# A two-layer graph kernel on 4096 nodes: the adjacency matrix is turned by VectorE's 32x32 transpose, and TensorE sums its rows in the first three turns

## The reference

```python
h = maximum(layernorm(x), 0)
weights = where(adj < 1.0, exp(-(1.0 / adj - 1.0) ** 2 / 0.5), 0.0)
x = x + weights @ (h @ W0 + B0)
h = maximum(layernorm(x), 0)
A_hat = adj + eye(4096)
d = sum(A_hat, axis=1) ** -0.5
x = x + relu((d[:, None] * A_hat * d[None, :]) @ (h @ W1.T))
```

## Time and profile before

| | |
|---|---|
| median of 3 runs | 651.94 us (651.78 to 652.38) |
| the profiled execution's span | 651.7 us |
| TensorE busy | 595.8 us (91%) |
| VectorE busy | 523.2 us (80%) |
| ScalarE busy | 479.0 us (73%) |
| HBM traffic | 157.67 MB, 242 GB/s over the span |
| granted TensorE clock, mean | 0.988 |

### The profile page before, as it was taken

The page is one execution under the profiler, slowest core; times in us unless marked ns, Lnnn a source line. Parts: engine busy times, 40 slices in busy tenths (PEclk is TensorE's granted clock), DMA queues, the critical chain, the costliest instruction groups (busy, mean ns, idle before and its releaser), DMA issues.

```text
span 651.7 us, 7163 instructions
## 1 busy us (share of the span) xinstructions
PE 595.8 (91%) x2307; PEld 337.1 (52%) x2307; DVE 523.2 (80%) x582; ACT 479.0 (73%) x357; POOL 65.2 (10%) x87
## 2 busy tenths in 40 slices
PE   2498988977979999999999999999999999999995
PEld 2475644544545555655555555554555554444432
DVE  4999999999999999999999994668763868531516
ACT  2799999999999999999999986476484665710000
POOL 2694000000000100010001000100000000001110
PEclk9799999999999999999999999999999999999999
DMA  9987685797886778677678883585744550527983
GB/s 258 388 322 252 236 293 194 263 313 261 271 284 229 253 264 303 252 237 266 223 272 312 300 337 130 186 283 194 268 168 152 202 221 0 205 83 301 301 295 104
DMA packets 54293, 157.67 MB, mean 242 GB/s; under 512 B 2561, under 2 KB 11010, under 8 KB 43778
## 3 DMA queue, kind: packets, MB, share of 16 engines
q1 hardware_dynamic: 48370, 114.43, 50.8%
q0 software_dynamic: 5904, 42.99, 18.0%
HBM read 112.33 MB, written 45.09 MB: 242 GB/s over the span
## 4 chain that ended last, share of the span: by engine, by line
PE 58%; DVE 22%; ACT 8%; issue 8%; DMA 3%; DVEq 0%; SPq 0%; ACTq 0%; POOL 0%; POOLq 0%
PE acc L381 18%; PE acc_late L420 11%; PE acc_once L397 11%; PE turned_ps L364 9%; PE turned_ps L519 6%; DVE rowpart L659 6%; DVE wt L680 5%; DVE wt L673 4%; DMA late<-adj_t_spill 3%; ACT wt L586 2%; PE side L420 2%; ACT wt L580 2%; ACT kept L569 2%; ACT wt L574 2%; DVE msg L779 1%
## 5 line engine op out<-in xcount | busy, mean ns | idle before, releaser
L381 PE MATMUL acc<-wt,msg 128*128 128x512 f32 x512 | 231.8, 596 | 20.4 <-ACT wt L586 20.4
L569 ACT COPY kept<-turned_ps 128x1024 f32<-128x1024 f32 x128 | 124.0, 1027 | 75.5 <-PE turned_ps L364 73.6
L680 DVE SCALAR_TENSOR_TENSOR wt<-wt 128x2048 f32<-128x2048 f32 x64 | 146.3, 2286 | 20.8 <-ACT wt L580 20.7
L381 PEld LDWEIGHTS acc<-wt,msg 128*128 128x128 f32 x512 | 93.8, 190 | 126.9 <-issue 101.9
L659 DVE TENSOR_REDUCE rowpart<-raw 128x4 f32<-128x2048 f32 x64 | 145.8, 2278 | 7.7 <-DMA raw<-in_adj_dram 7.7
L673 DVE SCALAR_TENSOR_TENSOR wt<-kept 128x2048 f32<-128x2048 f32 x64 | 146.2, 2284 | 5.0 <-ACT kept L569 5.0
L364 PEld LDWEIGHTS turned_ps<-ident,raw 128*128 128x128 f32 x1024 | 119.8, 144 | 36.7 <-issue 29.8
L364 PE MATMUL turned_ps<-ident,raw 128*128 128x128 f32 x1024 | 126.9, 279 | 9.6 <-DMA raw<-in_adj_dram 9.4
L586 ACT ACTIVATE wt<-wt 128x2048 f32<-128x2048 f32 x64 | 123.2, 1926 | 15.7 <-DVE wt L680 15.7
L574 ACT ACTIVATE wt<-wt 128x2048 f32<-128x2048 f32 x64 | 124.3, 1943 | 0.1
L580 ACT ACTIVATE wt<-wt 128x2048 f32<-128x2048 f32 x64 | 122.8, 1919 | 0.0
(11 more groups left out here) (74 smaller groups left out, 216.2 us busy)
## 6 DMA issues: line engine op xcount, KB each, us to landing
raw<-in_adj_dram SPq DMA_DIRECT2D x64, 1024.0 KB, 5.7
adj_t_spill<-kept SPq DMA_DIRECT2D x41, 1024.0 KB, 7.1
late<-adj_t_spill POOLq DMA_DIRECT2D x41, 1024.0 KB, 5.3
x<-in_x_dram SPq DMA_DIRECT2D x4, 512.0 KB, 7.7
out_dram<-fin SPq DMA_DIRECT2D x8, 256.0 KB, 3.2
w_sb<-in_L_gnn_W_dram SPq DMA_DIRECT2D x2, 64.0 KB
b_row<-in_L_gnn_B_dram SPq DMA_DIRECT2D x1, 0.5 KB
```

The lines of the kernel that those rows point to most:

```text
L381: mm = nc.tensor.matmul(acc0[:], msg[:, c * T + q, :], wt[:, p % WTS, q, :], start=(p % G == 0 and q == 0), stop=(p % G == G - 1 and q == ...
L569: nc.scalar.copy(kept[:, p % KEPT, q:q + 2, :], turned_ps[:, q:q + 2, :]).then_inc(copied, 1)
L680: nc.vector.scalar_tensor_tensor(out=v, in0=v, scalar=-2.0, in1=v, op0=ALU.add, op1=ALU.mult).then_inc(quad_done, 1)
```

## The change

The whole schedule is written anew. `adj` is now read in pairs of blocks (32 pairs of 2 MB, 64 units). Of a group of 1024 rows a pair takes 16 runs of 256 columns into each partition, and each quarter of the partitions (32 of them) has its own transfer, so a pair is four transfers of 512 KB in pieces of 1 KB. VectorE's transpose, which turns 32 x 32 squares within 32 partitions, then writes a turned block into `kept` directly: the transposes on TensorE, the banks `turned_ps` and ScalarE's copies are gone. There are two pair slots `raw` in place of four block slots, and six `wt` slots in place of four.

The row sums are split. In turns 0 to 2 TensorE multiplies each `kept` block with a matrix of ones of 32 columns, four products into four quarters of one PSUM bank (`sum_tiles`), and ScalarE and TensorE bring the sums into place once a turn. From turn 3 on VectorE reduces a pair at once (`row_sum`). The square of 1/adj - 1 is made on ScalarE (`square`) for every unit except the odd ones of turns 0 to 2, which VectorE does as before (`quad`). ScalarE also takes over the copy `x1t`. On VectorE the masked copy (`cut`) comes right behind the transpose in turns 0 to 2, and at the end of the step, behind the chain's work, from turn 3 on.

The order of the columns changes with the turn. 28 blocks are multiplied straight from `kept`, 35 are written out and read back, 20 of them in the turns: 1, 2, 3, 4, 5 and 5 in turns 2 to 7. The sums of layer two stay in six PSUM banks instead of being added into `mixed`. In the tail 16 blocks are multiplied, with seven slots for read-back blocks, four of which are halves of `raw`. The loops are unrolled.

```diff
-RAW, KEPT, WTS = 4, 4, 4
...
+RAW, KEPT, WTS, LATE = 2, 4, 6, 3
+LAG = 3
...
+ORDER = [[0, 1, 2, 3, 4, 5, 6, 7]]
+for turn_row in range(1, G):
+    young = turn_row - 1
+    ORDER.append([c for c in range(G) if c // 2 != young // 2] + [young ^ 1, young])
...
+JOBS = {17: [(0, 0)], 25: [(0, 1)], 28: [(1, 1)],
+        33: [(0, 2)], 35: [(1, 2)], 38: [(2, 2)],
+        41: [(0, 3)], 43: [(1, 3)], 45: [(2, 3)], 47: [(3, 3)],
+        48: [(0, 4)], 49: [(1, 4)], 51: [(2, 4)], 53: [(3, 4)], 55: [(4, 4)],
+        56: [(1, 5)], 57: [(2, 5)], 59: [(3, 5)], 61: [(4, 5)], 63: [(5, 5)]}
+TAIL = [(2, 6), (3, 6), (4, 6), (5, 6), (6, 6), (0, 5), (0, 6), (1, 6),
+        (2, 7), (3, 7), (4, 7), (5, 7), (6, 7), (7, 7), (0, 7), (1, 7)]
...
+PE_SUMS = 3
...
+def squared_by_dve(u):
+    return u < PE_SUMS * G and u % 2 == 1
...
-        adj_blocks = adj.rearrange("(g a p) (c j) -> g c p a j", a=T, p=P, j=ROWS)
...
+        adj_parts = adj.rearrange("(R e h i) (C q w) -> R h C q i e w", e=16, h=2, i=B, C=C4, q=Q)
...
-            def load(t, p, n):
+            def load(n):
+                g = n // C4
                 if n >= RAW:
-                    sp.wait_ge(cut_done, t.blocks(p - RAW + 1))
-                sp.dma_start(raw[:, p % RAW], adj_blocks[t.row + p // G, ORDER[p % G]]).then_inc(raw_loaded[p % RAW], 16)
-            def store(t, p):
-                sp.wait_ge(copied, t.blocks(p + 1, 2))
-                sp.dma_start(spill[t.row, 1 + ORDER[p]], kept[:, p % KEPT]).then_inc(spilled[p % KEPT], 16)
-            def turn(t, last=False):
-                for p in range(G):
-                    if not (last and p + AHEAD >= G):
-                        load(t, p + AHEAD, t.first * G + p + AHEAD)
-                    if stored(t.known)[p]:
-                        store(t, p)
+                    if n - RAW >= PE_SUMS * C4:
+                        sp.wait_ge(summed, n - RAW + 1 - PE_SUMS * C4)
+                    sp.wait_ge(turned, 2 * (n - RAW + 1))
+                for q in range(Q):
+                    sp.dma_start(raw[q * B:(q + 1) * B, n % RAW],
+                                 adj_parts[g // 2, g % 2, col(2 * n) // 2, q]).then_inc(raw_loaded[n % RAW], 16)
...
+            def store(u):
+                sp.dma_start(spill[u // G, col(u)],
+                             kept[:, u % KEPT].rearrange("p k i -> p (k i)")).then_inc(spilled[u % KEPT], 16)
...
+            load_x(0)
+            load(0)
...
+            for u in range(UNITS):
+                if spills(u):
+                    sp.wait_ge(turned, u + 1)
+                    store(u)
+                if u % 2 == 1 and u // 2 + RAW < PAIRS:
+                    load(u // 2 + RAW)
...
+            for j, (r, c) in enumerate(LOADED):
+                slot = late_slot(j)
+                u = r * G + ORDER[r].index(c)
+                before = slot_before(j)
+                if before is not None:
+                    pool.wait_ge(late_done, before + 1)
...
+                pool.wait_ge(spilled[u % KEPT], 16 * spill_count(u))
+                pool.dma_start(late_tile(slot).rearrange("p k i -> p (k i)"),
+                               spill[r, c]).then_inc(late_loaded[slot], 16)
...
-            def turn_tile(t, p, q):
...
-                    pe.wait_ge(copied, t.blocks(p - 1, 2) + q // 2 + 1)
-                for a in range(T):
-                    last = nc.tensor.transpose(turned_ps[:, q, a * P:(a + 1) * P],
-                                               raw[:, p % RAW, a, q * P:(q + 1) * P], ident[:])
-                if q % 2 == 1:
-                    last.then_inc(turned, 1)
...
+            def mix_once(u):
+                g, c = u // G, col(u)
+                pe.wait_ge(turned, u + 1)
...
+            def sum_tiles(u):
+                pe.wait_ge(turned, u + 1)
+                bank = sum_bank[u // G]
+                for k in range(T):
+                    mm = nc.tensor.matmul(bank[k * B:(k + 1) * B, :], ones[:], kept[:, u % KEPT, k, :],
+                                          start=(u % G == 0), stop=(u % G == G - 1))
+                mm.then_inc(tiles_summed, 1)
...
+            for u in range(UNITS):
+                g, idx = u // G, u % G
+                if g == 0 and idx % 2 == 0:
+                    turn_h0(idx // 2)
+                    multiply_msg(idx // 2)
+                if 1 <= g <= PE_SUMS and idx == 2:
+                    turn_sums(g - 1)
+                if g > PE_SUMS and idx == 1:
+                    sum_quads(g - 1)
+                if g < PE_SUMS:
+                    sum_tiles(u)
+                if at_once(u) and idx < G - 1 and not (g >= 6 and idx == 0):
+                    mix_once(u)
+                if g >= 1 and idx == 4:
+                    turn_x1(g - 1)
+                if u >= LAG:
+                    multiply_weights(u - LAG)
+                if g >= 1 and idx == 6:
+                    multiply_support(g - 1)
+                for i, (r, c) in enumerate(JOBS.get(u, [])):
+                    mix_late(first_job(u) + i, mix[r], r == 0 and c == 0, (r, c) in ((0, 4), (1, 5)))
+                if g >= 6 and idx == 0:
+                    mix_once(u)
+                if g >= 1 and idx == 5:
+                    turn_hid(g - 1)
+                if g >= 1 and idx == G - 1:
+                    mix_once(u)
...
+            for t, (r, c) in enumerate(TAIL):
+                if t == 0:
+                    sum_quads(G - 1)
+                if t < LAG:
+                    multiply_weights(UNITS - LAG + t)
+                if t == 4:
+                    turn_x1(G - 1)
+                if t == 5:
+                    turn_hid(G - 1)
+                if t == 6:
+                    multiply_support(G - 1)
...
+            def square(u):
+                v = wt[:, u % WTS]
+                act.wait_ge(inv_done, u + 1)
+                nc.scalar.activation(v, v, ACT.Square, bias=-1.0).then_inc(square_done, 1)
+            def weigh(u):
+                v = wt[:, u % WTS]
+                if squared_by_dve(u):
+                    act.wait_ge(quad_done, dve_squares(u))
+                    nc.scalar.activation(v, v, ACT.Exp, scale=-2.0, bias=-2.0).then_inc(wt_done, 1)
+                else:
+                    act.wait_ge(square_done, act_squares(u))
+                    nc.scalar.activation(v, v, ACT.Exp, scale=-2.0).then_inc(wt_done, 1)
+            def copy_sums(g):
+                act.wait_ge(tiles_summed, G * (g + 1))
...
+                nc.scalar.copy(in_tiles(hid_t[:]), by_tile(sum_bank[g][:])).then_inc(sums_copied, 1)
...
+            def copy_x1t(g):
+                act.wait_ge(acc0_done, (g + 1) * G)
+                nc.scalar.copy(in_tiles(x1t[:]), by_tile(acc0[:])).then_inc(x1t_copied, 1)
...
+            for u in range(UNITS):
+                g, idx = u // G, u % G
+                log(u)
+                if u >= 1 and not squared_by_dve(u - 1):
+                    square(u - 1)
+                if g >= 1 and idx == 6:
+                    log_pows(g - 1)
+                invert(u)
+                if u >= 1:
+                    weigh(u - 1)
+                if g == 0 and idx in (1, 3, 5):
+                    std_rows((idx + 1) // 2)
+                    copy_h0((idx + 1) // 2)
+                if 1 <= g <= PE_SUMS and idx == 1:
+                    copy_sums(g - 1)
+                if g >= 1 and idx == 3:
+                    copy_x1t(g - 1)
+                if g >= 6 and idx == 0:
+                    evict(g - 6)
+                if g >= 1 and idx == 6:
+                    exp_pows(g - 1)
+                    copy_hid(g - 1)
...
+            def turn(u):
+                n, h = u // 2, col(u) % 2
+                if u % 2 == 0:
+                    dve.wait_ge(raw_loaded[n % RAW], 64 * (n // RAW + 1))
+                if u >= KEPT:
+                    v = u - KEPT
+                    if spills(v):
+                        dve.wait_ge(spilled[v % KEPT], 16 * spill_count(v))
+                    if at_once(v):
+                        dve.wait_ge(once_done, once_count(v))
+                dst = kept[:, u % KEPT].rearrange("p k (e i) -> p e k i", i=B)
+                src = raw[:, n % RAW].rearrange("p e (k h i) -> p e k h i", k=T, h=2)[:, :, :, h, :]
+                nc.vector.transpose(dst, src).then_inc(turned, 1)
+            def row_sum(n):
+                g, jp = n // C4, n % C4
+                if g >= PE_SUMS + 2 and jp == 0:
+                    dve.wait_ge(quads_summed, g - 1)
+                dst = rowpart[:, g % 2, :, :, jp].rearrange("p a q -> p q a")
+                src = raw[:, n % RAW].rearrange("p (q a) w -> p q a w", q=Q)
+                nc.vector.tensor_reduce(dst, src, AX_X, ALU.add).then_inc(summed, 1)
+            def cut(u):
+                v = kept[:, u % KEPT]
+                dve.wait_ge(turned, u + 1)
+                if u >= WTS:
+                    dve.wait_ge(acc0_done, u - WTS + 1)
```

(97 more changed lines are left out.)

816 lines of the change are left out of this document (327 added, 489 removed), and 6 rows, old and new, of the table LATE.

## The result

The changed kernel takes 666.27 us (median of 4, 660.71 to 667.09), the kernel before on the same chip 651.86: a ratio of 1.020, 95% interval 1.017 to 1.024. It is 2% slower, where I had forecast 636 us and 2.4% faster. The time lies inside the stated range of 603 to 672 us, but on the other side of the kernel before. The profiled execution spans 665.3 us.

A forecast was written before the change was run, and what follows sets the result against it. It took TensorE, VectorE and ScalarE as full in turn 4, only TensorE from 350 us on. Stretches 143.3 + 2 x 63.3 + 64.1 + 67.6 + 71.0 + 74.5 + 88.4 = 635.5, forecast 636 us, range 603 to 672.

The forecast's parts named there:

- the chain of x1: In step 5 of turns 4 to 7, VectorE's cut behind x1's work fits in ScalarE's step 4, 0.9 us to spare.
- The wait in step 7: Turns 4 to 7: ScalarE's next logarithm waits 5.3 us for the cut behind `make_support`, making turn 4 64.1 us.
- its excess: TensorE's block work between mark and next `turn_x1` beyond 40.2 us lengthens turns 4 to 7 by 0, 3.5, 6.9, 10.4.
- The loads: Pair loads of `adj`: five pairs take 50 us; with spills and read-backs 63.3 us a turn, pacing turns 2 and 3.
- half-rate bound of 189: Loads into 32 partitions at 189 GB/s: a pair takes 11.1 us, a turn 44.4 + 23.3 = 67.7 us.
- this rival: Half-rate loads: pairs at 189 GB/s make turns 2 to 5 67.7 us each, 658 us in all, slower; chance 0.18.
- VectorE's transpose at 2.2 to 2.3 start to start: VectorE's transpose of each unit was taken at 2.20 us, like its other 2048-wide instructions; two passes would be 4.4.
- no other tables: ScalarE's square may need other tables, 1.28 us a load, 133 us in all; the prediction took nothing for it.
- the ones-sums hidden: TensorE's 24 ones-sums, 0.86 us a unit side by side or 3.43 one behind another, taken as hidden beside loads.
- the tail within 1.7 us: After the last mark: 75.5 us of blocks, 5.2 small products and output transposes, 0.5 wait, 7.2 to the end: 88.4.
- The fast-loads rival: Pair loads pass at 360 GB/s like the rest; first mark at 128 us, 604 us in all; chance 0.20.
- The clock: TensorE idles 2 us in a step of turns 3 and 4, possibly lowering its granted clock; counted within the waits.

## Why the prediction was wrong

**The step that failed** is this: "In step 5 the chain of x1 [...] fits in ScalarE's step 4 with 0.9 to spare." I took the lengths of the chain's own instructions and started it as soon as VectorE was ready. It starts when TensorE turns `x1t`, and TensorE comes to that behind a block and a read-back block (3.43 each at full clock; 8.3 for both here, since the first ran in part at a reduced clock) that themselves wait for the copy at the end of ScalarE's step 3. In place of 0.9 us to spare, ScalarE waited 7.21 in turn 4, and in step 5 of turns 3, 5, 6 and 7 it waited 3.85, 5.81, 7.99 and 11.42. The run with step 5's cut alone moved gives 25.7 us back, of which 22.9 lie in the turns where it acts, and the one with the earlier copy shows the wait at 0.31: shown.

**The wait in step 7** was right in kind and in size, 5.60 against 5.3, in turns 3 to 6. Taking it out gave only 8.5 us, not 5 x 5.3 = 26.5. In the turns with many read-back blocks TensorE is nearly full anyway (72.60 of 76.50 in turn 7), which the prediction had for its excess; and the step 5 wait stays, and in turn 5 grows from 5.81 to 7.87.

**The loads** were sized too cheap for this execution. I took 210 GB/s for the pairs. In turn 2, with 23.3 us for spills and read-backs at 360 as in the prediction, 8.39 MB in 68.0 - 23.3 us is 188 GB/s, by the prediction's way of counting its half-rate bound of 189. To the first mark it is 3.1 us, in turn 2 4.7. The same count gives 218 GB/s for the 61.7 us of turn 2 in the kernel with early cuts, so 188 is the low end of a range that holds my 210. Firmer is the start, where nearly only quarter transfers run: 195 to 197 GB/s at a full queue. The Trainium skill's 189 GB/s for 32 partitions ("Door 1: The DMA port swizzle", SBUF — State Buffer) is close to that. The 67.7 us a turn that the prediction estimated from it is close to the 68.0 of turn 2 here, but not to the 61.7 there. And as the pace of turn 3 in my sum, and of turns 3 to 5 in this rival, the loads were wrong: full-span transfers changed nothing there. The rival's 658 us came near the result for half of the right reason.

**What was right.** VectorE's transpose at 2.2 to 2.3 start to start; no other tables (one table load in the whole kernel); the ones-sums hidden (their omission gave nothing), at 1.06 us a unit at full clock, near my 0.86; the tail within 1.7 us; TensorE as the bound from turn 5 on, once the waits are gone. The fast-loads rival put the first mark at 128 us; with full-span transfers it came at 131.4.

**What came near by luck.** Turns 5 to 7 are within 3.0 us of my 67.6, 71.0 and 74.5. Those figures held the wait of step 7 but not that of step 5. With the late cuts of both steps the turns took 2.8, 3.0 and 2.0 more than them, with neither (62.2, 68.3 and 71.7) 5.4, 2.7 and 2.8 less, so the nearness does not confirm my working. Two slips in the prediction's sums are too small to matter: 8 x 7.2 is 57.6 and not 57.8, which makes its 64.1 a 63.8, and the terms named for the chain of x1 add up to 5.7 of a step's 7.2, which would leave 1.5 and not 0.9.

**The clock** was counted within the waits, with 2 us of idle time in a step of turns 3 and 4. TensorE idled 11.42 us in turn 4, the granted clock of turns 3 and 4 was 0.91 and 0.88, and 1.5 us of the chain's delay in turn 4 is the first block at a reduced clock (5.07 us against 3.60).

**Adding it up.** 607.4 us without either cause, against 652.6 before: what the change takes from the engines is worth 45 us. The half-rate loads take 22.6 to 26.7 of them back, the late cuts 32.2 to 36.3 (each taken away alone, and behind the other): 607.4 + 22.6 + 36.3 = 666.3. The sum closes because it is made of differences between the same runs; what it shows is that each cause costs about the same with and without the other.

**What stays open.** Up to its second mark the kernel with early cuts runs the same order of instructions as the changed kernel, and its turn 2 took 61.7 us against 68.0, at the same share (1.05) and 287 against 264 GB/s. So do the two with one cut moved, and theirs took 63.2 (step 5) and 66.5 (step 7). The executions of kernels with quarter transfers in plain order differ by 4 to 10 us, those with full-span ones by 0.8 to 1.6. Why the rate at a full queue differs between executions I did not try, and of the 32.2 us of the early cuts some 6 may be this, and of the 25.7 of step 5's cut some 5.

## What to carry to other kernels

When a work item is placed behind a chain on one engine, follow the chain back over every engine until it closes: here ScalarE waited for VectorE, it for TensorE, and TensorE for a copy that stood at the end of ScalarE's own step, and each piece by itself seemed to fit. Put the instruction that feeds the busiest engine ahead of the chain in its step; here moving one cut gave 26 us, 23 of them in the turns where it acts. Transfers into a quarter of the partitions paid nearly twice the queue time here (170 against 302 GB/s a full share) and slowed what shares the queue. If the layout demands them, try interleaving the halves of the partitions in small pieces: here the order gave 11.6 us and the smaller pieces another 9.5.

## What the runs showed of the hardware

- Quarter-partition transfers slow the others too. Only the loads' span of partitions was changed (and with it which rows of `adj` a transfer reads), and spills of 128 partitions landed after 6.6 us instead of 14.0, read-backs on the other queue after 5.2 instead of 10.1.
- Two transfers of 512 KB to different halves of the partitions hardly help each other at the start (203 against 197 GB/s from 16 to 32 us, 207 against 195 from 10 to 15). That agrees with the Trainium skill ("Can I just issue two DMAs to hit both halves?", SBUF — State Buffer: they serialize). With pieces of 128 KB in alternating halves it was 220 GB/s a full share, and 236 from 10 to 15 us. The section says that only a transfer over all 128 partitions reaches all ports; in whole kernels alternating order and smaller transfers together still gave 21 us (634.06 to 612.97).
- After 11.42 us of idle time TensorE's first block took 5.07 us instead of 3.60. The granted clock was 0.93 in the first part of the idle time, 0.50 in the rest, 0.71 during that block and 1.00 behind it, so part of the block ran at the lower level, 1.2 GHz. The wait cost TensorE a second time.

```profile
313.40:318.00 4.60, 0.00 (x0) 0.00 (x0) 4.57 (x3) 4.60 (x3) 0.00 (x0) 0.93 1.01 429
318.00:324.70 6.70, 0.00 (x0) 0.00 (x0) 6.70 (x3) 6.70 (x6) 0.00 (x0) 0.50 1.12 203
324.70:329.70 5.00, 4.92 (x9) 2.21 (x10) 1.31 (x1) 5.00 (x3) 0.00 (x0) 0.71 1.15 218
329.70:334.00 4.30, 4.30 (x15) 2.10 (x14) 0.24 (x1) 2.15 (x2) 0.42 (x1) 1.00 1.00 414
```

- Four f32 products of a 32-column ones matrix with 512 columns, one for each quarter of a bank's partitions, were busy 1.06 us a unit at a granted clock of 1.00 and 1.94 at 0.50; a block of as many full products takes 3.43 at 1.00.
